# Rounding of the rotary angles on ScalarE and GpSimd instead of VectorE, with squares, norm chain and transposes rearranged around it

## What is computed

```python
Bm = rmsnorm((x @ WB.T).reshape(B_, L, H, N), Bn_w) + B_bias      # H = 64 heads, N = 128
Cm = rmsnorm((x @ WC.T).reshape(B_, L, H, N), Cn_w) + C_bias
dt = softplus(x @ Wdt.T)
theta = (x @ Wth.T).reshape(B_, L, H, N // 2)
theta_cumsum = cumsum(theta * dt[..., None], axis=1)
Bm, Cm = rope(Bm, theta_cumsum), rope(Cm, theta_cumsum)           # x0*c - x1*s, x0*s + x1*c
# then a scan over time: h = alpha*h + beta*(B_prev x_prev) + gamma*(B x);  y = C h
```

## Time and profile before

| | |
|---|---|
| median of 3 runs | 3599.38 us (3589.8 to 3600.61) |
| profiled execution | 3601.3 us, of which the span is 3599.5 us |
| busy: PE, DVE, ACT, POOL | 2897.9, 2374.4, 1820.9, 1539.4 us |
| granted PE clock, mean | 0.882 |

### The profile page before, as it was taken

The page is one execution under the profiler, slowest core; times in us unless marked ns, Lnnn a source line. Parts: engine busy times, 40 slices in busy tenths (PEclk is TensorE's granted clock), DMA queues, the critical chain, the costliest instruction groups (busy, mean ns, idle before and its releaser), DMA issues.

```text
span 3599.5 us, 84310 instructions
## 1 busy us (share of the span) xinstructions
PE 2897.9 (81%) x28752; PEld 2199.6 (61%) x28752; DVE 2374.4 (66%) x3926; ACT 1820.9 (51%) x3740; POOL 1539.4 (43%) x1420
## 2 busy tenths in 40 slices
PE   5139957788888899999977999999899998279573
PEld 4128846466666657667654667676676676168462
DVE  5214224699999849889945988884888885243135
ACT  1016624566666356666614666663666672046331
POOL 3550050255555416655610555551455553510345
PEclk7559968889899899999978999998999998589785
DMA  9537755466665246556403666642666653467564
GB/s 387 197 123 254 255 163 179 142 183 184 177 184 176 77 139 171 164 162 171 134 3 119 173 172 172 171 134 68 170 172 171 172 160 115 158 206 254 175 205 138
DMA packets 311258, 605.54 MB, mean 168 GB/s; under 512 B 59136, under 2 KB 159616, under 8 KB 310016
## 3 DMA queue, kind: packets, MB, share of 16 engines
q1 hardware_dynamic: 286464, 535.63, 48.9%
q0 software_dynamic: 24576, 67.14, 5.6%
HBM read 446.25 MB, written 155.32 MB: 167 GB/s over the span
## 4 chain that ended last, share of the span: by engine, by line
PE 53%; DVE 19%; issue 10%; another core or an unknown queue 7%; ACT 4%; DMA 4%; POOL 1%; DVEq 1%; SPq 1%; POOLq 0%; ACTq 0%
PE bank L63 15%; PE bank L568 7%; PE bank L1327 4%; DVE tmp L1275 3%; PE bank L1197 3%; PE bank L1393 3%; DVE xbc L1251 3%; DMA rc_in<-decay_t 3%; PE bank L581 2%; PE bank L559 2%; PE bank L1391 2%; PE cs_sn L581 2%; PE bank L1367 2%; DVE rot L1275 2%
## 5 line engine op out<-in xcount | busy, mean ns | idle before, releaser
L63 PE MATMUL bank<-xh,wb 128*128 128x512 f32 x2048 | 685.4, 416 | 73.1 <-ACT btr L1342 43.2
L644 DVE TENSOR_TENSOR hh<-sg,bank 128x96 f32<-128x96 f32 x384 | 97.5, 254 | 596.4 <-ACT sg L619 372.6
L63 PEld LDWEIGHTS bank<-xh,wb 128*128 128x128 f32 x2048 | 373.3, 192 | 190.4 <-ACT btr L1342 63.9
L1206 ACT ACTIVATE xbc<-bank,norm_w 128x512 f32<-128x512 f32 x512 | 350.7, 685 | 240.8 <-PE bank L63 234.1
L1295 POOL TENSOR_TENSOR sq<-cst,rho 128x512 f32<-128x512 f32 x128 | 133.5, 1043 | 742.8 <-DVE xbc L1251 411.3
L1283 POOL TENSOR_TENSOR rot<-rot,tmp 128x512 f32<-128x512 f32 x256 | 341.8, 1335 | 238.3 <-DVE tmp L1275 238.3
L568 PE MATMUL bank<-wgu,xgT 128*128 (+1 forms) x1536 | 343.7, 350 | 107.6 <-issue 68.2
L63 PE MATMUL bank<-xl,wb 128*128 128x512 f32 x1024 | 408.5, 399 | 0.0
L1284 POOL TENSOR_TENSOR rot<-rot,tmp 128x512 f32<-128x512 f32 x256 | 358.7, 1401 | 0.0
L568 PEld LDWEIGHTS bank<-wgu,xgT 128*128 128x128 f32 x1536 | 261.0, 204 | 118.5 <-issue 118.1
L1275 DVE SCALAR_TENSOR_TENSOR rot<-xbc,bias,cs_sn 128x1024 f32<-128x1024 f32 x256 | 325.4, 1271 | 8.4 <-DVE xbc L1251 6.8
(11 more groups left out here) (277 smaller groups left out, 6084.7 us busy)
## 6 DMA issues: line engine op xcount, KB each, us to landing
wb<-watt_dram SPq DMA_DIRECT2D x96, 1024.0 KB, 7.7
rr_bc<-rr_dram SPq DMA_DIRECT2D x128, 512.0 KB
yd<-ys SPq DMA_DIRECT2D x96, 512.0 KB
wd<-w_down SPq DMA_DIRECT2D x384, 96.0 KB
watt_dram<-wb SPq DMA_DIRECT2D x32, 1024.0 KB, 5.4
dt_bc<-row_dram SPq DMA_DIRECT2D x256, 128.0 KB
al_bc<-row_dram SPq DMA_DIRECT2D x256, 128.0 KB, 3.2
xd<-xg SPq DMA_DIRECT2D x12, 2048.0 KB, 23.7
```

What stands on the lines that cost most here:

```text
L63: ins = e.matmul(dst, a, m, start=start and c == 0, stop=stop and c == n - 1, skip_group_check=not (start and stop))
L1206: e.activation(xbc[j % 4][:, i, :], of(i)[:, :], ACT.Copy, scale=norm_w[:, i:i + 1])
```

## The change

The second step of the rounding leaves DVE. ACT adds MAGIC and then, in a second operation in place, subtracts it; POOL subtracts `cum`, behind `own_pool`. `T_pe` then waits for `cum` alone. The matmuls of the squares write four row groups of 32 with 256 columns each instead of two with 512, so that the square root covers 100 rows by 256, and the norm chain's DMAs go as two halves. `R_act` stands ahead of `T_act2`, `R_sp1` ahead of the other SP items of the turn. The first transposes stand ahead of `G_pe` and wait for the first half of `F_pool` alone. In sequence 0 the weight splits of ACT and DVE stand earlier in the turn, and the load of theta weights stands at the end of SP's turn.

```diff
 def T_pe(e, m, j, cnt):
-    e.wait_ge(e_nfr.sem, e_nfr.at(m))
+    e.wait_ge(e_cum.sem, e_cum.at(m))
-def T_dve2(e, m, j):
+def T_pool2(e, m, j):
     e.wait_ge(e_rnd.sem, e_rnd.at(m + 1))
-    e.wait_ge(e_cs.sem, e_cs.at(m))
+    e.nop(nofuse=True)
     e.wait_ge(e_cum.sem, e_cum.at(m + 1))
-    e.scalar_tensor_tensor(nfr[:, :], W[2][:, :], MAGIC, cum[:, :], ALU.subtract, ALU.subtract).then_inc(e_nfr.sem, 1)
+    e.tensor_tensor(nfr[:, :], nfr[:, :], cum[:, :], ALU.subtract).then_inc(e_nfr.sem, 1)
 def T_act2(e, m, j):
...
-    e.activation(W[2][:, :], cum[:, :], ACT.Identity, bias=magic[:, 0:1]).then_inc(e_rnd.sem, 1)
+    e.wait_ge(e_cs.sem, e_cs.at(m))
+    e.activation(nfr[:, :], cum[:, :], ACT.Identity, bias=magic[:, 0:1]).then_inc(e_rs.sem, 1)
+    e.wait_ge(e_rs.sem, e_rs.at(m + 1))
+    e.activation(nfr[:, :], nfr[:, :], ACT.Identity, bias=minus_magic[:, 0:1]).then_inc(e_rnd.sem, 1)
 def ss_pe(e, m, j):
     for eo in range(2):
-        for ty in range(2):
-            first = 30 - 28 * (1 - ty) - 2 * (j % 2)
-            ins = e.matmul(SSB[32 * ty:32 * ty + 32, :], one_hot[:, first:first + 32], sq4[:, 2 * ty + eo, :], ...)
+        for half in range(2):
+            for ty in range(2):
+                first = 30 - 28 * (1 - ty) - 2 * (j % 2)
+                g = 64 * half + 32 * ty
+                ins = e.matmul(SSB[g:g + 32, 0:HALF], one_hot[:, first:first + 32], sq4[:, 2 * ty + eo, half * HALF:(half + 1) * HALF], ...)
 def R_act(e, gm):
-    e.activation(stdr, SSB[0:36, :], ACT.Sqrt, scale=1.0 / NS, bias=eps_nm[0:36, 0:1]).then_inc(e_sr.sem, 1)
+    e.activation(stdr, SSB[0:100, 0:HALF], ACT.Sqrt, scale=1.0 / NS, bias=eps_nm[0:100, 0:1]).then_inc(e_sr.sem, 1)
 def R_sp1(e, gm):
-    e.dma_start(rc_in[:, :], stdr[NORM_ROWS, :].rearrange("r (c w) -> r c w", w=32)).then_inc(a_r1.sem, 16)
+    for h in range(2):
+        e.dma_start(rc_in[CL * h:CL * h + CL, :], stdr[NORM_ROWS[h], :].rearrange("r (c w) -> r c w", w=32)).then_inc(a_r1.sem, 16)
 def R_sp2(e, gm, par):
-    e.dma_start(rr_dram[par].rearrange("r (c w) -> (r c) w", w=32), rc[:, :]).then_inc(a_r2.sem, 16)
+    for h in range(2):
+        dst = rr_dram[par][:, h * HALF:(h + 1) * HALF].rearrange("r (c w) -> r c w", w=32)
+        e.dma_start(dst, rc[CL * h:CL * h + CL, :]).then_inc(a_r2.sem, 16)
 def F_pool(e, n, j, types):
+    if ty == 0:
+        ins.then_inc(e_Rb.sem, 1)
 def tr_pe(e, p, j, eo, x):
     if eo == 0:
-        e.wait_ge(e_R.sem, e_R.at(p + 1))
+        e.wait_ge(e_Rb.sem, e_Rb.at(p + 1))
 def turn_pe(e, b, it, first, last):
     if K:
+        tr_pe(e, p, jp, 0, 0)
         G_pe(e, p, jp)
-        tr_pe(e, p, jp, 0, 0)
 def turn_act(e, b, it, first, last):
     T_act3(e, n, j)
+    if RG:
+        R_act(e, gm + 1)
     if T:
         T_act2(e, n + 1, j + 1)
-    if RG:
-        R_act(e, gm + 1)
+    if is_first(b) and not last:
+        wb_high_act(e, q + 4, j, it * 2 + j // 2 + 2)
+    if is_first(b) and not (last and j >= 2):
+        th_high_act(e, q + 2, j, it * 2 + j // 2 + 1)
...
-    if is_first(b) and not last:
-        wb_high_act(e, q + 4, j, it * 2 + j // 2 + 2)
-    if is_first(b) and not (last and j >= 1):
-        th_high_act(e, q + 3, j + 1, it * 2 + (j + 1) // 2 + 1)
 def turn_pool(e, b, it, first, last):
     own_pool(e, n + 1, q + 1)
+    T_pool2(e, n + 1, j + 1)
 def turn_dve(e, b, it, first, last):
-    if T:
-        T_dve2(e, n + 1, j + 1)
...
     R_dve(e, gm + 1)
+    if is_first(b) and not last:
+        wb_low_dve(e, q + 4, j)
+    if is_first(b) and not (last and j >= 2):
+        th_low_dve(e, q + 2, j)
     F_dve3(e, n, j, q, [0])
     F_dve3(e, n, j, q, [1])
...
-    if is_first(b) and not last:
-        wb_low_dve(e, q + 4, j)
-    if is_first(b) and not (last and j >= 1):
-        th_low_dve(e, q + 3, j + 1)
 def turn_sp(e, b, it, first, last):
...
-    th_store_sp(e, q + 2, j)
+    th_store_sp(e, q + 1, j + 1)
+    if RG:
+        R_sp1(e, gm + 1)
     dt_sp(e, q + 2, j + 2)
     end_sp(e, q + 2, j + 2)
-    if not (last and j >= 1):
+    if not is_first(b) and not (last and j >= 1):
         th_load_sp(e, b, q + 3, j + 1)
     wb_load_sp(e, b, q + 4, j)
-    if RG:
-        R_sp1(e, gm + 1)
     al_sp(e, q + 2, j + 2)
     if RG:
         R_sp2(e, gm + 1, (j // 2 + 1) % 2)
         R_sp3(e, gm + 1, (j // 2 + 1) % 2)
+    if is_first(b) and not (last and j >= 1):
+        th_load_sp(e, b, q + 3, j + 1)
```

More of the change, by code:

```diff
@@ L96, in build @@
         eps_ln, eps_nm, magic, half_pi = (sb(n, [P, 1]) for n in ("eps_ln", "eps_nm", "magic", "half_pi"))
+        minus_magic = sb("minus_magic", [P, 1])
         mean_w = sb("mean_w", [P, P])
@@ L186, in build @@
         norm_w = sb("norm_w", [P, 4])
-        stdr = decay_t[0:36, :, :, :].rearrange("p k q a -> p (k q a)")
-        NORM_ROWS = slice(28, 36)
+        HALF = SEQ // 2
+        stdr = sb("stdr", [100, HALF])[:, :]
+        NORM_ROWS = [slice(28, 36), slice(92, 100)]
         rc_in, rc = sb("rc_in", [P, 32]), sb("rc", [P, 32])
@@ L195, in build @@
         ones = one[:, :].to_broadcast([P, SEQ])
-        ytmp = cum[0:CL, 0:SEQ // 2]
+        ytmp = sb("ytmp", [CL, SEQ // 2])[:, :]
         afr = ths
@@ L1194, in ss_pe @@
             for eo in range(2):
-                for ty in range(2):
-                    first = 30 - 28 * (1 - ty) - 2 * (j % 2)
-                    ins = e.matmul(SSB[32 * ty:32 * ty + 32, :], one_hot[:, first:first + 32], sq4[:, 2 * ty + eo, :],
-                                   start=j % 2 == 0 and eo == 0, stop=j % 2 == 1 and eo == 1, skip_group_check=True)
+                for half in range(2):
+                    for ty in range(2):
+                        first = 30 - 28 * (1 - ty) - 2 * (j % 2)
+                        g = 64 * half + 32 * ty
+                        ins = e.matmul(SSB[g:g + 32, 0:HALF], one_hot[:, first:first + 32], sq4[:, 2 * ty + eo, half * HALF:(half + 1) * HALF],
+                                       start=j % 2 == 0 and eo == 0, stop=j % 2 == 1 and eo == 1, skip_group_check=True)
             ins.then_inc(e_ssm.sem, 1)
@@ L1394, in Y_pe, with Y_dve @@
             ins.then_inc(e_Y.sem, 1)
-        def Y_dve(e, p, q2, n, nfr_done):
+        def Y_dve(e, p, q2, n):
             e.wait_ge(e_Y.sem, e_Y.at(p + 1))
@@ L1528, in turn_dve @@
                 if j % 2 == 1 and not (first and j == 1):
-                    Y_dve(e, n - 2, q - 3, b * (NP // 2) + it * 2 + (j - 3) // 2, n + 1 + T)
+                    Y_dve(e, n - 2, q - 3, b * (NP // 2) + it * 2 + (j - 3) // 2)
                 F_dve1(e, n, j, b * NB + it + 1)
@@ L1554, in turn_sp @@
                     wb_load_sp(e, b, q + 4, j)
-                if is_first(b) and not (last and j >= 2):
-                    th_store_sp(e, q + 2, j)
+                if is_first(b) and not (first and j == 0) and not (last and j == 3):
+                    th_store_sp(e, q + 1, j + 1)
+                if RG:
+                    R_sp1(e, gm + 1)
                 if not (last and j >= 2):
@@ L1593, in pairs_pe @@
             Y_pe(e, p - 1, j - 1, (b + 1) * (NP // 2) - 1)
+            tr_pe(e, p, j, 0, 0)
             G_pe(e, p, j)
-            tr_pe(e, p, j, 0, 0)
             z_pe(e, b, 2)
@@ L1627, in pairs_pool @@
                 e.memset(acc4, 0.0).then_inc(e_az.sem, 1)
+            T_pool2(e, N, 0)
             e.wait_ge(e_x12.sem, e_x12.at(b + 1))
@@ L1650, in pairs_dve @@
             K_dve2(e, p, j, (b + 1) * NB)
-            Y_dve(e, p, NP - 2, (b + 1) * (NP // 2) - 1, N + NP)
+            Y_dve(e, p, NP - 2, (b + 1) * (NP // 2) - 1)
         def pairs_sp(e, b):
@@ L1779, in _ @@
             e.memset(magic[:, :], MAGIC)
+            e.memset(minus_magic[:, :], -MAGIC)
             e.memset(half_pi[:, :], float(np.pi / 2))
```

16 lines of the change are left out of this document (6 added, 10 removed).

## The result

The changed kernel takes 3703.3 us (median, 3699.0 to 3728.0) where the kernel before, run beside it, takes 3594.6: a ratio of 1.032, 95% interval 1.028 to 1.036. It is slower by 3.2%; 3548 was forecast, with a range of 3475 to 3635. The profiled execution took 3728.0 us, 126.7 more than the one before.

What follows compares the result with a forecast made beforehand. The norm chain's loop was to bound sequences 1 to 3, DVE sequence 0. Savings of 25 (sequence 0), 18 (1) and 8 (2 and 3), together 51 on 3601.3, gave 3550; the median 1.9 lower, 3548 us; range 3475 to 3635.

Steps and rivals of the forecast that it cites:

- The loop of the norm chain: From S (square root's end, odd turn) through SP's queue to the next S: 29.8 us, the bound in sequences 1 to 3.
- the broadcasts: Two broadcasts of 512 KB each in SP's queue: 6.0 us after the write, plus 0.1 for a wakeup.
- the megabyte: Weights ahead of the reciprocals' write in SP's queue: 6.5 us with `al_bc`, between 5.4 and 8.6.
- the scatter: Transfer that slowed the weights before: it would come earlier than they do in the new order, so 6.5 us was taken.
- the norm chain overruns: Rival, chance 0.20: the megabyte takes 8.6 us as before, two turns of sequences 1 to 3 take 31.9, total 3642.
- if they take 32, it is the time of the megabyte: Sign: two turns at 32 us would mean the step that failed is the megabyte's time in SP's queue.
- Sequence 0: DVE stays the bound there; two turns gain 1.7 us net, 25 us over 15 periods.
- held by ACT: Rival, chance 0.11: ACT's early weight split waits for its load; sequence 0 gains nothing or loses 1.3, total 3593.
- Sequence 1: Two turns fall from 31.0 to 29.8 us, alike with sequences 2 and 3; 18 us gained over 15 periods.
- PE at 28.0: PE alone would need 28.0 us per two turns: 26.8 of work, 1.0 waiting for ACT's copy, 0.2 of other waits.
- DVE's wait for `rr_bc`: Sign: before `F_dve1` of even turns in sequences 2 and 3, DVE idles 1.5 to 3 us for this DMA.
- The squares: PE's squares, four row groups at a time: 0.92 us instead of 1.84, a gain of 0.92 per turn.

Runs made afterwards that it cites:

- a4: The changed kernel with sequence 0's B/C weight splits on ACT and DVE back in their old places; 1.022 of the kernel before.
- c4: c3 with `G_pe` ahead of the first transposes again; 0.991 of the kernel before.
- b3: The changed kernel unaltered, run again with a second profile; 1.029 of the kernel before.
- e1: The changed kernel unaltered, run again on another chip; 1.030 of the kernel before.
- d3: c4 run once more, unaltered; 0.993 of the kernel before.
- a1: The changed kernel with `R_sp1` again behind the load of the weights in SP's turn; 1.009 of the kernel before.
- b4: The changed kernel with the weights issued behind the broadcasts in odd turns of sequences 1 to 3; 1.061 of the kernel before.
- c3: a4 with `R_sp1` behind the weights in sequences 1 to 3 only; 1.004 of the kernel before.
- a3: The kernel before with only the squares in four groups, square root over 100 x 256 and transfers in halves; 1.0025 of the kernel before.
- c1: The kernel before with only the first transposes moved ahead of `G_pe`; 1.013 of the kernel before.
- c2: The kernel before with only the rounding changed (second step on ACT, subtraction on POOL); 1.0005 of the kernel before.
- d1: c4 with squares and norm chain as in the kernel before (two groups, whole transfers); 0.995 of the kernel before.

## Why the prediction was wrong

*The loop of the norm chain* was the forecast's bound and is the changed kernel's. The terms of it, by the period shown above:

| from S | forecast | measured |
|---|---|---|
| weights issued | 5.9 | 5.8 |
| weights, `al_bc` and the write, to the issue of the broadcasts | 6.5 + 0.9 | 8.2 |
| to the start of `F_dve1` | 6.0 + 0.1 | 7.8 |
| `F_dve1` to the next S | 10.4 | 10.4 |
| the loop | 29.8 | 32.2 |

The step that failed is the time of SP's queue behind S: +0.8 on the megabyte and the write, +1.7 on the broadcasts. The forecast took 6.5 for the megabyte between ends of 5.4 and 8.6, because the scatter would not fall on it. It did not: the scatter's packets are those of the software queue q0, and over the transfer of the weights the kernel before has some (first line, 2165.5 to 2172.5) and the changed kernel none (second, the only queue there from 2217 to 2223.5):

```profile
q0 software_dynamic: 48, 0.13, 4.9%
```

```profile
q1 hardware_dynamic: 811, 1.56, 77.0%
```

It is so in every period of sequence 2: 32 packets of 4 KB before, none after. The queue moved at 247 GB/s there and not at the 301 of the earlier trace rows; why is open. The broadcasts were misread: the window chosen in the earlier trace rows ends at 2180.2, and the forecast took that for their landing. The next window of the kernel before shows that the queue went on at the same rate, and packets of 2048 bytes were still in it:

```profile
2180.20:2181.70 1.50, 1.39 (x68) 1.28 (x67) 1.46 (x3) 0.69 (x1) 0.61 (x3) 1.00 1.07 219
```

By the packets of this size, which are those of the broadcasts and of the next `dt_bc` mixed with them, they ran to some 7.5 us behind the issue in both kernels (to 2182 before, to 2232 after). So they cost the same before and after; their last 1.5 us were hidden then, and the chain had 1.5 us to spare, not 3. With the two terms right the sum gives 32.2 in all of sequences 1 to 3. That is the period of the rival *the norm chain overruns* (31.9, price 3642, chance 0.20), and its condition is met: weights, write and broadcast take 16.0 us, not 13.4. But its reason was the scatter on the megabyte, and that did not happen; two thirds of the excess are the broadcasts, whose time no rival doubted. Its number was met by another way, and the prediction's own sign ("if they take 32, it is the time of the megabyte") points at the smaller of the two terms.

*Sequence 0* was to gain 25 us by DVE and lost 12. DVE's busy time did fall, by 47 us in the window, but the bound had moved. The place of the early splits was the failed step here: the rival *held by ACT* is in the waits, 43 us for the load of `w_att`, and a4 without it takes 34.8. That was mechanism and place of the rival; at 0.11 it was given too little, and it came together with an overrun of the norm chain, to which it was held to be an alternative. The gain itself was there to be had: without the early splits and with the transposes behind `G_pe`, two turns take 34.2 us (c4).

*Sequence 1* was taken to be equal to sequences 2 and 3. It takes 34.7, 2.4 more than they do. Of eleven periods eight take 31.7 to 35.1 us, which is the loop again, and three 39 to 42. In those PE stands without a releaser:

```profile
1473.33 0.38 PE L1404 MATMUL bank<-x1p,sq 128*64 128x16 f32 x2
1478.36 0.29 PE L1406 MATMUL bank<-st,rot 128*64 128x16 f32 x1 [4.65 <-issue]
```

The window of sequence 1 has 34 packets in the queue of instruction fetches, that of sequence 2 has 8. In b3 they are 24, and two turns take 34.1; in e1 they are 7, and two turns take 32.2 (385.8/12). So some 37 us of the profiled 126.7 go with them, in an execution that was 25 us above the median, and e1, which hasn't got them, is still at 1.030. Why instructions are fetched again inside this loop, and whether they are PE's, is open. d3 has 25 of them too. More than 8 are seen only with the four-group squares, but not in every such run (a1, a4, b4, c3 and e1 have 7).

*PE at 28.0* was met in single periods only (27.9 in a1, 28.1 in a3), and full clock was assumed throughout. The last column is an estimate: the clock's cost is taken as the window's shortfall from 1.00 times the period, which holds where PE is the bound:

| sequence 2 | two turns | clock | at full clock |
|---|---|---|---|
| before | 30.05 | 1.00 | 30.05 |
| a1, a3 | 30.2 | 0.96 | 29.0 |
| c1, transposes first | 30.7 | 0.96 | 29.5 |
| c2, rounding alone | 29.8 | 0.99 | 29.5 |
| d1, two groups | 29.9 | 0.99 | 29.6 |
| d3, four groups | 29.4 | 0.97 | 28.6 |

By this estimate the four groups save 1.0 us of two turns at full clock, and half is given back; the transposes save nothing (29.5 in c1 and c2) and lose 0.9 in these windows. With both, as in a1, PE would need 29.0 at full clock, 1.0 more than forecast. That the clock takes the rest is read from the records; no run held the clock fixed, so it is argued, not shown.

*Single steps.* DVE's wait for `rr_bc` was to be 1.5 to 3 us in a period; it is 2.8 (33.7/12). The squares: 1.10 to the start of what follows (2223.66 to 2224.76) where the earlier trace rows has 1.84, against a forecast 0.92. Four groups do overlap, but 0.74 us per turn are saved, not 0.92. The square root: 0.47 against 0.45. The two magic operations: 0.71 and 0.72 against 0.68. POOL's subtraction: 1.34 against 1.25. The whole rounding is worth nothing (c2): in sequences 2 and 3 PE is the bound, and in sequence 0, where DVE was busy for 97% of the time, its busy time fell by 6.3 us of the 16.4 and the period not at all. What held sequence 0 in c2 wasn't found. The idle time before the reciprocal was to go, and it did (no wait for `rc_in` in sequence 2), but nothing waited for that gain. The Trainium skill's rule ("DMA: Bandwidth & Descriptors", Rules for kernel authors) that splitting a transfer into partition halves isn't worth it: the trace agrees, write to next issue takes 2.7 us in halves (a3, the kernel before with the halves) and 1.6 whole.

## What to carry to other kernels

A small transfer at the end of a chain of waits should go ahead of a large one in the same queue only if both are still in time; ask for each order which of the two is late, and price the queue by bytes that will share it then, not by what it took before. When the order of a queue moves, the large transfer should be issued before the wait, not after it (a1, c3 and c4 against the changed kernel and b4). Time freed on TensorE can come back as a lower clock after the new idle time, so a gain has to be read from the period and not from the engine's sum. When a rival's number is met, look whether its reason was met too.

## What was not expected of the hardware

- In a3 the granted clock went from 0.96 to 0.50 behind five microseconds in which PE was busy 2.44. The kernel before, with 1.4 us of idle time per two turns in smaller pieces, ran at 1.00 throughout the window of sequence 2.
- Two transfers of 8 KB each for `rr_dram` need 1.36 us to issue where the whole needed 0.32, and the two halves of `rc_in` 1.44 where the whole needed 0.70.
- PE's stop of 4.65 us inside a burst of small matmuls, with nothing that released it, in a loop where 34 instruction packets are fetched instead of 8.
- The same pair of kernels gave 1.040 on one chip and 1.029 on another, the kernel before taking 3354 and 3599 us. Two turns of the loops are alike there (c2 against the earlier trace rows, 29.8 and 30.05 us in sequence 2); most of the 245 us lie in the FFN stages, about 105 ahead of the first square root and 119 behind the last (c2 against the kernel before), and their cause wasn't looked for.
